# Decoder layer on one core: the last product rows go from SBUF to SBUF, and the read-back of the others is issued one step earlier

## The reference

```python
def step(M, kv):
    k_t, v_t = kv
    v_pred = jnp.einsum('bf,bfd->bd', k_t, M)
    surprise = jnp.linalg.norm(v_t - v_pred, axis=-1, keepdims=True)
    delta = k_t[:, :, None] * v_t[:, None, :]
    M = M + eta_c[None, :, None] * surprise[:, :, None] * delta
    return (_ln2(M), None)
```

## Time and profile before

| | |
|---|---|
| median of 3 runs | 1955.6 us |
| the profiled execution's own time | 1955.59 us |
| its span | 1953.9 us |
| TensorE matmul busy | 1311.3 us (67%) |
| VectorE busy | 1370.8 us (70%) |
| ScalarE busy | 1133.0 us (58%) |
| GpSimd busy | 1030.3 us (53%) |
| SyncE's hardware queue q1, share of 16 engines | 23.2% |

### The profile page before, as it was taken

How to read it: one execution, slowest core, us unless ns; L and a number is a source line. 1 busy time by engine, 2 the same in 40 slices (tenths; PEclk the granted TensorE clock), 3 DMA queues, 4 the chain that set the end, 5 groups by cost and what they waited for, 6 DMA issues and landing times. The chain is left out here.

```text
span 1953.9 us, 60466 instructions
## 1 busy us (share of the span) xinstructions
PE 1311.3 (67%) x18195; PEld 1070.9 (55%) x18196; DVE 1370.8 (70%) x4870; ACT 1133.0 (58%) x3308; POOL 1030.3 (53%) x1566
## 2 busy tenths in 40 slices
PE   6999995888858729996654999100000786849990
PEld 5777773666646618995653677100000565639990
DVE  5999994877787754453555666499999577755574
ACT  4777772777746616774554555365556565626674
POOL 3666664455559967777862444011111453867663
PEclk9999996999989969997886999655555898969995
DMA  3333331311112213333443454200000422323343
GB/s 88 98 94 97 97 98 41 112 49 49 51 45 72 69 44 91 97 97 116 135 136 93 89 109 83 41 1 1 1 1 5 153 67 62 86 59 90 88 114 115
DMA packets 192277, 148.11 MB, mean 76 GB/s; under 512 B 19458, under 2 KB 179586, under 8 KB 191746
## 3 DMA queue, kind: packets, MB, share of 16 engines
q1 hardware_dynamic: 178818, 118.93, 23.2%
q0 software_dynamic: 13312, 27.49, 4.3%
HBM read 76.54 MB, written 61.34 MB: 71 GB/s over the span
## 5 line engine op out<-in xcount | busy, mean ns | idle before, releaser
L1035 PE MATMUL ffn_run_up_ps<-ffn_run_xt,ffn_run_w_now 128*128 128x128 f32 x1792 | 250.5, 284 | 47.3 <-DVE ffn_run_h L1163 19.9
L1005 POOL DMA_INDIRECT expert_outputs<-ffn_run_y_all,ffn_run_ids x224 | 219.0, 978 | 87.6 <-issue 45.2
L1035 PEld LDWEIGHTS ffn_run_up_ps<-ffn_run_xt,ffn_run_w_now 128*128 128x128 f32 x1792 | 225.8, 198 | 59.1 <-ACT ffn_run_xt L1071 30.2
L778 POOL DMA_INDIRECT tokens_by_expert<-ffn_x_all,ffn_dest x192 | 192.8, 1004 | 52.6 <-issue 45.5
L1779 PE MATMUL mixer_m_ps<-mixer_mine,mem_state_coef 128*64 128x64 f32 x4 | 0.5, 334 | 284.2 <-DVE mixer_off_in L1913 284.2
L1044 PE MATMUL ffn_run_y_ps<-ffn_weights,ffn_run_h 128*128 x1216 | 174.0, 277 | 0.7 <-DVE ffn_run_y_all L1180 0.5
L1511 POOL TENSOR_TENSOR recur_rho<-recur_var_eps_new,k_pack 128x1 f32<-128x1 f32 x64 | 34.9, 545 | 248.4 <-DVE recur_var_eps_new L1605 248.4
L1779 PEld LDWEIGHTS mixer_m_ps<-mixer_mine,mem_state_coef 128*64 128x64 f32 x4 | 0.3, 206 | 284.3 <-DVE mixer_ones L1911 284.3
L1044 PEld LDWEIGHTS ffn_run_y_ps<-ffn_weights,ffn_run_h 128*128 128x128 f32 x1216 | 155.5, 194 | 1.1 <-issue 1.1
L1072 ACT COPY ffn_run_w_now<-ffn_weights 128x512 f32 x224 | 139.4, 622 | 0.1
L382 POOL TENSOR_TENSOR self_k_ex<-self_kt,k_pack 128x256 f32<-128x256 f32 x128 | 75.9, 614 | 116.7 <-ACT self_kt L569 116.7
(11 more groups left out here) (335 smaller groups left out, 4697.6 us busy)
## 6 DMA issues: line engine op xcount, KB each, us to landing
ffn_run_x<-tokens_by_expert SPq DMA_DIRECT2D x56, 260.0 KB, 2.9
tokens_by_expert<-fill_zeros SPq DMA_DIRECT2D x32, 292.5 KB, 2.8
ffn_run_yg<-expert_outputs SPq DMA_DIRECT2D x16, 512.0 KB, 4.7
memory_rows<-products_row SPq DMA_DIRECT2D x16, 390.0 KB, 4.6
ffn_weights<-memory_rows SPq DMA_DIRECT2D x16, 390.0 KB
tokens_by_expert<-fill_zeros SPq DMA_DIRECT2D x32, 162.5 KB, 2.6
ffn_weights<-in_pack_ffn SPq DMA_DIRECT2D x1, 4112.0 KB, 14.8
self_turned<-in_x_turned SPq DMA_DIRECT2D x64, 64.0 KB, 1.8
```

Source lines behind the costliest of these rows:

```text
L778: pool.indirect_dma_start(xs[h], bass.IndirectOffsetOnAxis(ap=self.dest[:, r, t:t + 1], axis=0), self.x_all[:, t, :], None)\
L1005: pool.indirect_dma_start(ys, bass.IndirectOffsetOnAxis(ap=ids[:, t:t + 1], axis=0), y_all[:, t, :], None)\
L1035: mm = nc.tensor.matmul(up_ps[t.slot(2)][:, c * P:(c + 1) * P], w_now[:, t.slot(2), c * P:(c + 1) * P], xt[:, t.slot(2), :], start=True, s ...
```

## The change

For the last four tiles the way through memory is gone. As soon as a row tile is ready, SyncE issues two *direct* transfers, one for each sequence: source 64 partitions x 780 bytes in `row`, destination one partition of `room`. All other groups keep store and read-back, but the read-back's offset goes from i - 5 to i - 4. The counts that SyncE waits for at the end are adapted.

```diff
             def step(i):
                 t = i + -1
-                if t.exists() and t.c % 4 == 3:
+                if t.exists() and t.c >= NT - 4:
+                    n, slot, uses = four(t)
+                    sp.wait_ge(row_ready, t.count())
+                    sp.wait_ge(row_copied, t.count())
+                    for b in range(2):
+                        sp.dma_start(room[2 * t.n + b:2 * t.n + b + 1, 0:S * ROW], row[b * S:(b + 1) * S, slot, t.c % 4, :]).then_inc(rows_back, 16)
+                elif t.exists() and t.c % 4 == 3:
                     n, slot, uses = four(t)
                     sp.wait_ge(row_ready, t.count())
                     sp.wait_ge(row_copied, t.count())
                     sp.dma_start(rows_v[n], row[:, slot, :, :]).then_inc(stored[slot], 16)
-                t = i + -5
-                if t.exists() and t.c % 4 == 3:
+                t = i + -4
+                if t.exists() and t.c % 4 == 3 and t.c < NT - 4:
                     n, slot, uses = four(t)
                     sp.wait_ge(stored[slot], uses * 16)
                     sp.dma_start(room[bass.ds(n * 8, 8), 0:S * ROW], batch_v[n]).then_inc(rows_back, 16)
...
-            for c in range(-11, NT + 5):
+            for c in range(-11, NT + 1):
                 step(kind(0, c))
-            for s in stored:
-                sp.wait_ge(s, 16 * NT // 8)
-            sp.wait_ge(rows_back, 16 * NT // 4)
+            for n, s in enumerate(stored):
+                sp.wait_ge(s, 16 * (NT // 8 - n))
+            sp.wait_ge(rows_back, 16 * (NT // 4 - 1 + 8))
```

## The result

The changed kernel takes 1951.1 us (median of 22 runs) against 1954.4 us for the kernel before in the same sessions: ratio 0.9983, 95% interval 0.9975 to 0.9991. That is 3.4 us or 0.17% less; it is clear of no change, and inside the 0.2% within which the forecast called it the same. The profiled execution has a span of 1951.3 us.

A forecast was written before the change was run, and what follows sets the result against it. The 20 us hole between product rows and recurrence was taken as the bound. Store 14's landing, direct transfers, read-back 14 and the last pair summed to 1248.3 against 1247.1: net + 1.2 on 1955.6, so 1956.8 us, range 1948 to 1963.

The forecast's parts named there:

- the landing of store 14: End of the product stage: store 14 lands at 1234.8, before about 1224.8; R, the last product row's end, was 1229.73.
- the time that the six direct transfers hold read-back 14 up: Behind store 14 on 8 engines, transfers of tiles 60 to 62 add 5.2 us before read-back 14.
- what bounds: The hole of 20 us between VectorE's last product row and the recurrence; at most part of 17.35 us winnable.
- the mechanism of edit 1: In each round, a store's packets for 8 engines queue behind the read-back's pieces; stores land in about 11 us.
- Rival A: Nothing waits behind the read-back's pieces; stores land in 4.6 us as before; gain 9.1 us, 1946.5; chance 0.11.
- the price of edit 1: At the stage's end: read-backs one step earlier make store 14 land 10 us later.
- Rival C: Direct transfers: one partition takes no more than a piece does, 6.9 us per sequence; + 32 us, 1988; chance 0.02.
- The thirteen loops: From store 1 to store 14, read-back and store wait for each other: 10.8 us each, against a round of 10.7.
- The 0.6 us of stall in the first round: VectorE wants store 1's buffer at 1093.75, but it lands at 1094.4; later rounds add 0.1 us each.
- Rival B: The store and read-back loop becomes the bound at 11.1 us or more; at 11.2, 1962.0 us; chance 0.21.
- 0.87 us for a direct transfer on the loaded engines: Each direct transfer's half on the 8 loaded engines takes 0.87 us, 3.5 us a pair; low bound 0.15.
- what comes behind: After the six direct transfers: read-back 14 6.9 us, tile 63's pair 1.75, semaphore 1.2; from 1238.5 to 1248.3.

The follow-up runs named there:

- edit 1: Read-backs one step earlier (i - 4 for i - 5); run alone against the kernel before, all 16 groups by store and read-back: 1959.9 us, ratio 1.0029.
- the kernel with short pieces: The changed kernel with each read-back's eight destination partitions 4 apart instead of neighbours: 1941.9 us, ratio 0.9940 to the kernel before.
- edit 2: Eight direct transfers replace store 15 and read-back 15; run alone against the kernel before, read-backs left at i - 5: 1949.8 us, ratio 0.9970.
- three orders of the same transfers: The changed kernel, 1951.1 us; direct transfers with read-backs left at i - 5, 1949.8; the latter with read-back 14 between the pairs of tiles 61 and 62, 1951.7.

## Why the prediction was right or wrong

The range (1948 to 1963) holds 1951.1, and the chance for the same was the largest. But the number was 1956.8, 1.2 above before, and it is 3.4 below: the sign was wrong, and that the range holds the time is no merit of the sum. Two terms of the sum failed, the landing of store 14 and the time that the six direct transfers hold read-back 14 up; they are 5.5 us too much between them.

**Right: what bounds.** The hole was the only place; 3.2 us of it went and the time fell by 3.4. **Right: the mechanism of edit 1.** Stores stand behind the read-back's pieces on 8 engines and land in 10.0 us instead of 4.6 (11 was forecast); that is shown by the two humps, and by the kernel with short pieces, where they land in 6.1. Rival A, that nothing waits behind the pieces, is out. **Half right: the price of edit 1.** Alone it costs 5.2 us. Beside edit 2 it costs nothing that the hole shows (16.88 us with it, 16.89 without); the sum charged it there with "a store 14 that lands 10 us later". Rival C wanted the stage to end 32 us later, and is out.

**Wrong: the landing of store 14, "1094.4 + 13 x 10.8 = 1234.8".** It was to be 5.1 us after R (1234.8 − 1229.73) and was 2.5 (1234.60 − 1232.08): 2.6 too late. Most of that is the first round, 12.35 us from the load's issue to the landing of store 1. Store 1, issued at 1085.39, has

```profile
DMA to landing us min/median/max: 9.5/9.5/9.5
```

so it landed at 1094.9, 10.8 us after the load's issue at 1084.10: 1.5 less. By the packet records the pieces began 1.9 us after that issue (2.55 in the sum), and from the end of the last piece to the landing it was 2.1 us (2.9 in the sum, with 2.5 as its low bound). The thirteen loops add 0.7: from 1094.9 to 1234.60 it is 10.75 us each, not 10.8. The other 0.3 is the slightly longer way from store 0 to the last row. The loop itself, from read-back to read-back, was 10.6, 10.4 and 10.9 us in the last three rounds, where no load stands ahead; before them it stayed just below the round, since SyncE waited for a store only twice. The 0.6 us of stall in the first round and 0.1 in each later one did not come: VectorE never waits for a store. Rival B used the same chain, and did not come about.

**Wrong: 0.87 us for a direct transfer on the loaded engines.** The sum let read-back 14 start 3.7 us after the landing of store 14, behind six of them. The DMA view of the changed kernel from 1233.0 to 1237.2, slices of 0.105 us, has the start:

```profile
GB/s 141 134 112 104 45 45 30 15 15 22 22 15 15 8 15 22 15 30 22 22 22 15 22 490 973 498 951 15 15 0 1018 104 67 0 0 0 52 104 75 8
```

The first pieces begin at 1235.4 and the last at about 1236.2, 0.8 to 1.6 us after 1234.60. Bytes are booked densely up to 1233.5 and thinly from there. From 1233.5 to 1235.4 the view has 67 packets, 15 of them small:

```profile
DMA packets 67, 0.04 MB, mean 21 GB/s; under 512 B 15, under 2 KB 67, under 8 KB 67
```

That leaves at most 52 of the 192 packets that the six transfers have on the 8 engines, so most had gone before read-back 14 was issued, in time that was waited for store 14 anyway. The sum had put all six behind store 14. That is 2.9 us too much. The size was too high as well: a transfer has four packets on an engine, at 0.15 us each 0.6 us, not 0.87.

**Slightly low: what comes behind.** From read-back 14's first bytes to the last semaphore (wait from 1236.10, 10.1 us long, so 1246.2) it is 10.8 us, the sum had 1238.5 to 1248.3, 9.8; pieces of 7.8 us instead of 6.9 are about as much. Together − 2.6 − 2.9 + 1.0 = − 4.5: R + 14.1 measured, R + 18.6 forecast. With 3.2 less hole instead of 1.2 more the account closes to 0.1 us.

What stays open: why three orders of the same transfers end within 0.3 us of each other (holes 16.9, 16.9, 17.1), and why a read-back next to direct transfers has longer pieces. That the transfers share one line on 8 engines fits the first; the sum of their times was not measured by itself.

## What to carry to other kernels

Before moving a transfer in a queue, look at the longest packet that it puts in front of the others: on the engines it uses, what was issued later waited for it here (stores 10.0 us instead of 4.6). And before cutting a transfer out, look at how long each packet takes against the same size elsewhere in the trace: pieces that took 6.9 us for 50 KB, next to 22 GB/s in another load, were a sign to try other destination partitions, and a new address for them won more than the shortened path. Where a sum multiplies a small difference (10.8 against 10.7) by thirteen rounds, its sign is not known. And ask of each transfer whether it runs in time that is waited anyway: here most of the direct transfers did, and the sum had put them behind the wait.

## What the runs showed of the hardware

In a kernel's last read-back, eight pieces of 49,920 B took 6.9 us each into eight neighbouring partitions (6.0 in the kernel with edit 1 alone), 3.9 into partitions 16 apart, and 2.4 into partitions 4 apart, with the same source and the same number of engines. Next to direct transfers they took 7.8 to 8.0 us into neighbours and up to 4.3 into partitions 4 apart; why is not shown. A store whose engines are free landed in 4.4 us, behind the long pieces in 10.0, and behind those of partitions 4 apart in 6.1. Packets of 780 B from 64 partitions into one took 0.15 us on average when several transfers wrote neighbours at once, 0.06 when they wrote partitions 4 apart, 0.05 when a single pair wrote neighbours, and 0.04 in a store to memory.
